# Attention score matmuls on 64-row halves of the TensorE array, per head, with a single K copy

## What is computed

```python
x = x + attn0(layernorm(x))        # 16 heads of width 8, softmax(q k^T / sqrt(8)) v, then @ wo.T + bo
x = x + ffn0(layernorm(x))         # silu(x wg^T) * (x wu^T), hidden 384, then @ wd^T (int weights / 127)
x = x + attn1(layernorm(x))        # 16 heads of width 8; q and k RMS-normalised per head and scaled
x = x + moe1(layernorm(x))         # x @ base_w^T + b + softmax-gated LoRA experts (8 experts, rank 8)
```

## Time and profile before

| | us |
|---|---|
| time, median of 3 runs (2163.48 to 2167.84) | 2164.41 |
| span of the profiled execution | 2165.0 |
| busy TensorE, its weight loads | 1980.4, 763.2 |
| busy VectorE, ScalarE, GpSimd | 1638.9, 1431.8, 434.7 |
| chain that ended last: PE 62%, issue 15%, DVE 10%, DMA 5%, POOL 4% | |
| busy share of the 16 DMA engines by the main queue | 23.2% |

### The profile page before, as it was taken

One profiled execution on the slowest core, in us unless ns is written; L12 is line 12 of the kernel. 1 busy time (PEld: TensorE's weight loads), 2 busy tenths in 40 slices (PEclk: granted clock), 3 DMA queues, 4 the chain that ended last, 5 costly groups with the idle time before them and its releaser, 6 DMA issues.

```text
span 2165.0 us, 38228 instructions
## 1 busy us (share of the span) xinstructions
PE 1980.4 (91%) x10706; PEld 763.2 (35%) x10706; DVE 1638.9 (76%) x3602; ACT 1431.8 (66%) x2921; POOL 434.7 (20%) x571
## 2 busy tenths in 40 slices
PE   3958999999999999999999999999999999999785
PEld 1223333333333333333333333333333333333332
DVE  5638888787887878778787877878787778888471
ACT  2615676676766767676776767677676767676643
POOL 2112121131212113121211312121121213121200
PEclk8858999999999999999999999999999999999977
DMA  5112314040311404031130404114050412302020
GB/s 108 55 25 58 87 34 122 18 135 19 111 44 39 116 17 137 17 116 39 46 109 17 138 16 119 36 46 109 17 138 17 118 36 62 94 20 72 18 63 16
DMA packets 162656, 140.94 MB, mean 65 GB/s; under 512 B 38761, under 2 KB 144050, under 8 KB 162482
## 3 DMA queue, kind: packets, MB, share of 16 engines
q1 hardware_dynamic: 162482, 139.29, 23.2%
HBM read 77.38 MB, written 55.57 MB: 61 GB/s over the span
## 4 chain that ended last, share of the span: by engine, by line
PE 62%; issue 15%; DVE 10%; DMA 5%; POOL 4%; ACT 2%; SPq 2%; DVEq 0%; POOLq 0%; ACTq 0%
PE ps L1159 17%; PE ps L1134 14%; PE ps L1144 14%; DVE neg_max L881 5%; PE ps L1209 4%; PE ps L1110 3%; PE ps L1173 3%; PE ps L1182 2%; PE ps L1214 2%; DMA k_stack<-k_rows 2%; ACT probs L661 1%; DVE bn L858 1%; DMA k_rows<-kp 1%; PE ps L1221 1%; DMA rden_all<-rden_rows 1%
## 5 line engine op out<-in xcount | busy, mean ns | idle before, releaser
L881 DVE TENSOR_REDUCE neg_max<-ps 128x1 f32<-128x512 f32 x2048 | 1323.5, 681 | 231.2 <-PE ps L1134 194.0
L661 ACT ACTIVATE probs<-ps 128x512 f32<-128x512 f32 x2048 | 1093.8, 599 | 347.2 <-PE ps L1144 345.6
L1134 PE MATMUL ps<-k_stack,q_stack 96*128 96x512 bf16 x2048 | 798.7, 392 | 80.2 <-DVE neg_max L881 51.2
L1144 PE MATMUL ps<-q_stack,k_stack 128*128 128x512 bf16 x2048 | 782.7, 385 | 16.8 <-ACT probs L661 14.0
L1159 PE MATMUL ps<-probs,v_aug 128*32 128x512 f32 x4096 | 548.8, 608 | 0.4
L1144 PEld LDWEIGHTS ps<-q_stack,k_stack 128*128 128x128 bf16 x2048 | 202.9, 100 | 441.8 <-ACT probs L661 244.9
L1134 PEld LDWEIGHTS ps<-k_stack,q_stack 96*128 96x128 bf16 x2048 | 202.3, 99 | 371.7 <-DVE neg_max L881 192.4
L561 POOL TENSOR_TENSOR o_raw<-o_raw,rden_all 128x512 f32<-128x512 f32 x64 | 81.4, 1272 | 580.7 <-DMA rden_all<-rden_rows 580.7
L1159 PEld LDWEIGHTS ps<-probs,v_aug 128*32 128x32 f32 x4096 | 80.7, 108 | 184.4 <-ACT probs L661 102.3
L667 ACT ACTIVATE xn<-x,shift,rstd 128x128 f32<-128x128 f32 x192 | 80.7, 486 | 49.4 <-POOL shift L544 49.3
L578 POOL TENSOR_TENSOR ht<-up,gs 128x512 f32<-128x512 f32 x48 | 60.9, 1268 | 257.3 <-ACT up L642 257.3
(11 more groups left out here) (109 smaller groups left out, 1487.5 us busy)
## 6 DMA issues: line engine op xcount, KB each, us to landing
q_stack<-q_rows SPq DMA_DIRECT2D x128, 192.0 KB, 3.4
k_stack<-k_rows SPq DMA_DIRECT2D x128, 192.0 KB, 4.3
rden_all<-rden_rows SPq DMA_DIRECT2D x64, 256.0 KB
q_rows<-qp SPq DMA_DIRECT2D x32, 384.0 KB, 2.6
k_rows<-kp SPq DMA_DIRECT2D x32, 384.0 KB, 3.0
q_rows<-qp SPq DMA_DIRECT2D x32, 256.0 KB, 2.9
k_rows<-kp SPq DMA_DIRECT2D x32, 256.0 KB, 3.0
x_in<-in_L_attn_x SPq DMA_DIRECT2D x16, 256.0 KB, 2.8
```

The source lines that it names most:

```text
L661: act.activation(probs[:, u % RING, :], ps[:, bank_of(l, u), :], ACT.Exp).then_inc(exps, 1)
L881: dve.tensor_reduce(neg_max[l][:, pair // 2, col:col + 1], ps[:, BANKS + bank_of(l, n), :], AX.X, ALU.max, negate=True).then_inc(max_taken, 1)
L1134: pe.matmul(ps[:, BANKS + bank_of(l, 2 * n + e), :], q_stack[l][0:QROWS, pair, tok:tok + 128], k_stack[l][e][0:QROWS, pair, :], start=True ...
L1144: pe.matmul(ps[:, bank_of(l, u), :], k_stack[l][e][:, pair, tok:tok + 128], q_stack[l][:, pair, :], start=True, stop=True).then_inc(scores, 1)
```

## The change

- One K copy: `k_stack[l]` holds head e = 0 in rows 0 to 49 (48 and two rows of ones) and head e = 1 in rows 64 to 113; `q_stack[l]` likewise, with each head's maximum rows behind its own 48.
- A score matmul reads only its head's rows: 48 (max) or 50 (attend), from row 0 or from row 64. The max units take e = 1 first, the attend units e = 0 first, so the halves alternate in TensorE's order: A low, M high, A high, M low.
- The zeroing and the ones rows on VectorE go; GpSimd fills both K stacks with bfloat16 ones (two memsets, at the start of its queue).
- `max_rows` needs two DMAs, one per head, and `m_in` counts 32 for each quarter.
- The pieces can be issued in parts, but `sub_slots` gives all parts of a piece the same half-step, behind the second score pair of the step as before. Only the form of q0, k0, g and u changes: two matmuls of 256 columns in the place of one of 512 (float32, each two instructions).

```diff
+ONE_PAIR = 1.001937866210937500
-QROWS = 2 * KROWS
+AROWS = KROWS + MROWS
+HALF = 64
...
+PARTS_OF = {"q0": 2, "k0": 2, "v0": 2, "v1": 2, "rt": 2, "pr0": 4, "pr1": 4, "dn": 4, "out": 4, "qka": 2, "qkb": 2,
+            "g0": 2, "u0": 2, "g1": 2, "u1": 2, "g2": 2, "u2": 2}
+
+def sub_slots(name, at_step):
+    n = PARTS_OF[name] if name in PARTS_OF else 1
+    return [(2 * at_step + 1, k, k == n - 1) for k in range(n)]
...
-        k_stack = [[sb(f"k_stack{l}{e}", [128, PAIRS, SEQ], BF16) for e in (0, 1)] for l in (0, 1)]
+        k_stack = [sb(f"k_stack{l}", [128, PAIRS, SEQ], BF16) for l in (0, 1)]
...
-                        sp.dma_start(stacks[e][KROWS * e:KROWS * e + KROWS, 4 * half:4 * half + 4, :], src
+                        sp.dma_start(stack[HALF * e:HALF * e + KROWS, 4 * half:4 * half + 4, :], src
                                      ).then_inc(stack_in[l][half], 16)
...
-                sp.dma_start(q_stack[l][QROWS:QROWS + 2 * MROWS, 2 * quarter:2 * quarter + 2, :],
-                             m_parts[l][quarter % 2][:, :]).then_inc(m_in[l][quarter], 16)
+                for e in (0, 1):
+                    sp.dma_start(q_stack[l][HALF * e + KROWS:HALF * e + AROWS, 2 * quarter:2 * quarter + 2, :],
+                                 m_parts[l][quarter % 2][16 * e:16 * e + 16, :]).then_inc(m_in[l][quarter], 16)
...
             pool.memset(mid_bias[:, EXPERTS:], 0.0)
+            for l in (0, 1):
+                pool.memset(k_stack[l][:, :, :].rearrange("p a b -> p (a b)").bitcast(F32), ONE_PAIR).then_inc(k_ones, 1)
...
-                        for t in (*k_stack[1], q_stack[1]):
-                            pool.memset(t[:, :, :].rearrange("p a b -> p (a b)").bitcast(F32), 0.0).then_inc(k_zeros, 1)
...
-                    zero_stacks((*k_stack[0], q_stack[0]))
                     place_weights()
-                    set_ones(0)
                     clear_values(0)
...
                                 clear_values(1)
-                                dve.wait_ge(k_zeros, 3)
-                                set_ones(1)
...
-                pair, st, e = n // 8, (n // 2) % 4, n % 2
+                pair, st, e = n // 8, (n // 2) % 4, 1 - n % 2
...
+            def max_score(l, m, b):
                 base = 2 * STEPS * maxima_before(l, b)
+                n, e = m // 2, 1 - m % 2
+                if m % 32 == 0:
+                    pe.wait_ge(stack_in[l][m // 32], 64 * (b + 1))
+                need(pe, max_taken, free_at(l, m, b, base))
+                tok, pair, row = 128 * (n % 4), n // 4, HALF * e
+                pe.matmul(ps[:, BANKS + bank_of(l, m), :], q_stack[l][row:row + KROWS, pair, tok:tok + 128],
+                          k_stack[l][row:row + KROWS, pair, :], start=True, stop=True).then_inc(max_scores, 1)
...
-                pe.matmul(ps[:, bank_of(l, u), :], k_stack[l][e][:, pair, tok:tok + 128],
-                          q_stack[l][:, pair, :], start=True, stop=True).then_inc(scores, 1)
+                tok, pair, row = 128 * kt, 2 * group + pp, HALF * e
+                pe.matmul(ps[:, bank_of(l, u), :], k_stack[l][row:row + AROWS, pair, tok:tok + 128],
+                          q_stack[l][row:row + AROWS, pair, :], start=True, stop=True).then_inc(scores, 1)
...
+            def by_column(w, xt, half):
+                return pe.matmul(gen[:, 256 * half:256 * half + 256], w, xt[:, 256 * half:256 * half + 256],
+                                 start=True, stop=True)
```

More of the change, by code:

```diff
@@ L423, in stack_half @@
                     hold(scores, UNITS * attends_before(l, b - 1) + 32 * (half + 1))
-                for rows, stacks in ((q_rows[l], (q_stack[l], q_stack[l])), (k_rows[l], k_stack[l])):
+                for rows, stack in ((q_rows[l], q_stack[l]), (k_rows[l], k_stack[l])):
                     for e in (0, 1):
@@ L1168, in turn_norm, with by_token @@
                 return last
-            def by_token(dst, xt, w, more=None):
-                for t in range(TT):
+            def by_token(dst, xt, w, tiles, more=None):
+                for t in tiles:
                     last = pe.matmul(dst[:, t, :], xt[:, 128 * t:128 * t + 128], w, start=True, stop=more is None)
@@ L1176, in by_token, with project, piece @@
                 return last
-            def project(l, b):
-                pe.wait_ge(att_ready[l], 2 * b + 2)
-                for t in range(TT):
-                    for c in (0, 1):
-                        last = pe.matmul(gen4[:, t, :], o_raw[l][:, c, 128 * t:128 * t + 128], wo[l][:, c, :],
-                                         start=c == 0, stop=c == 1)
+            def by_column(w, xt, half):
+                return pe.matmul(gen[:, 256 * half:256 * half + 256], w, xt[:, 256 * half:256 * half + 256],
+                                 start=True, stop=True)
+            def project(l, t):
+                for c in (0, 1):
+                    last = pe.matmul(gen4[:, t, :], o_raw[l][:, c, 128 * t:128 * t + 128], wo[l][:, c, :],
+                                     start=c == 0, stop=c == 1)
                 return last
-            def piece(name, i, at, kind, b):
+            def piece(name, k, i, at, kind, b):
                 before = piece_before(kind, at, name)
-                if before is not None:
+                if k == 0 and before is not None:
                     pe.wait_ge(read[sem_name(before[0])], count(before[0], i + before[1]))
@@ L1192, in piece @@
                 elif name in ("q0", "k0"):
-                    pe.wait_ge(read["xt0"], b + 1)
-                    last = pe.matmul(gen, (wq if name == "q0" else wk)[:, :], xnt[0][:, :], start=True, stop=True)
+                    if k == 0:
+                        pe.wait_ge(read["xt0"], b + 1)
+                    last = by_column((wq if name == "q0" else wk)[:, :], xnt[0], k)
                 elif name == "v0":
-                    pe.wait_ge(read["xt0"], b + 1)
-                    last = by_token(gen4, xnt[0], wv[:, :])
+                    if k == 0:
+                        pe.wait_ge(read["xt0"], b + 1)
+                    last = by_token(gen4, xnt[0], wv[:, :], (2 * k, 2 * k + 1))
                 elif name == "v1":
-                    last = by_token(gen4, xnt[2], wqkv[:, 256:384])
+                    last = by_token(gen4, xnt[2], wqkv[:, 256:384], (2 * k, 2 * k + 1))
                 elif name[0] == "m":
@@ L1235, in piece @@
                 elif name == "out":
-                    last = by_token(gen4, xnt[3], w_base[:, :], more=(coef_t, w_lora[:, :]))
-                last.then_inc(written[sem_name(name)], 1)
+                    last = by_token(gen4, xnt[3], w_base[:, :], (k,), more=(coef_t, w_lora[:, :]))
+                return last
             def slot(kind, i, at):
@@ L1249, in slot @@
                             pe.wait_ge(read["k0"], 1)
-                            last = by_token(gen4, xnt[0], wv[:, :])
+                            last = by_token(gen4, xnt[0], wv[:, :], range(TT))
                         else:
```

103 lines of the change are left out of this document (43 added, 60 removed).

## The result

The changed kernel takes 2136.26 us (median; 2124.73 to 2143.32) where the kernel before, on the same chip, takes 2165.45 (2163.48 to 2167.84): a ratio of 0.986, 95% interval 0.9825 to 0.9889. It is 29 us faster; I had forecast 91. The profiled executions have spans of 2134.1 and 2165.0 us, a difference of 30.9.

A forecast was written before the change was run, and what follows sets the result against it. TensorE's order of issue was taken as the bound, VectorE close behind. Steady turns 72 us (5.0 each), start 6.7, Y 0 5.4 and ends 7 sum to 91 off 2165: 2073 us; range 2035 to 2165, the forecast's own 2035 to 2110.

The forecast's parts named there:

- Halves do not overlap: Rival: a score pair keeps 0.44 us and 46 drains a turn come on top; 2201 us, chance 0.12.
- The ring does not bind: Rival: the three score banks hold nothing up, each group costs its most loaded engine's sum; 1980 us, chance 0.07.
- dearer drains and more chain waits: Rival: pairs overlap, but whole-array/halves changes cost 0.2 us (2146 us), or DMA chains wait more; 2110 to 2170, chance 0.12.
- start and Y 0: VectorE's memsets for the K copies go: stack loads 6.7 us earlier, first Y slot's gate product 5.4 us earlier.
- (a): Eight light groups a turn: 0.36 us each less what VectorE's or a piece's small work fills; 1.4 us together.
- (b): Ten groups a turn with a piece behind PV, Y 4 and X 9 included: 0.06 to 0.26 us each, 1.8 together.
- (c): Four groups a turn with pieces at both steps (Y 7, 8, 9, 13): 0.3 us each, 1.2 together.
- (d): Eight groups a turn that VectorE paces already (Y 5, 6, 11, 12, 14, 15, X 6, 7): nothing gained.
- (e): X 0 and X 1, at the loop's turn: X 0 loses a 0.1 drain, X 1 saves 1.05; 0.95 us together.
- 0.4 for the projection pr0: Layer-0 projection in Y: 0.23 us of slack before a DMA chain getting only part of the gain; 0.4 lost a turn.
- second DMA, I take 0: Extra issue of 0.69 us on SP per quarter of the maxima: cost taken as 0, other end 20 us.
- the clock: Rival: TensorE, less busy, gets a lower clock; one more low stretch a turn would be 25 us; chance 0.03.

The follow-up runs named there:

- The run without overlap: Changed kernel with every score matmul on the low half of the rows, head 1's scores left out: 2303.64 and 2335.93 us.
- The runs without the chain: Both kernels with GpSimd multiplying by a constant tile, waiting only for the denominators' first DMA: 2095.56 us from the changed kernel, 2149.55 from the kernel before.
- the waits moved in both kernels: Reciprocal's rows issued earlier, GpSimd's layer-1 residuals reordered, second half of layer 1's stacks later: changed kernel 2107.23 us, kernel before 2151.62.

## Why the prediction was right, and where it was wrong

**Right, the mechanism.** Pairs at 0.22 to 0.23, starting together; the fourth pair held by the ring of three (I had named the maximum; the exponential holds it too, 963.06); a light group 2.55 where I had 2.48; score to PV still 0.31. *Halves do not overlap* was the rival that would have made the kernel slower. The run without overlap is slower, but not as I had priced it: by medians its turn is 0.8 longer than that of the kernel before (65.0 + 61.2 against 63.4 + 62.0), where I had 3.4 for the drains, and what makes it slow is a low clock that I had not priced. *The ring does not bind* falls by the earlier trace rows's counterpart: by it the fourth pair starts 0.66 behind the first, and its two scores started at 1.15 and 1.24.

**Right, the drains.** PV to a piece stays 1.00 and a piece to the next score grew by 0.09 to 0.12 (an up projection from 0.96 to 1.06, the layer-0 projection from 1.89 to 1.98), by 0.20 for one (v1, 0.89 to 1.09). So the change between whole array and halves costs about what I took; four instructions in the place of two showed nothing more. The measured time lies in the band of the rival *dearer drains and more chain waits* (2110 to 2170, chance 0.12): of its two halves the drains are out, and the chain waits came.

**Right, start and Y 0.** The first attend score came at 55.8 and not 62.4, 6.6 (6.7 predicted); slots Y 0 and X 0 together are 6.0 shorter (5.4 predicted, and a part of the 7 for the ends), and the slot behind them 0.7. The rest of those 7 did not come: what follows the steady part is 1.5 longer, with 12 us more at 1.2 GHz.

**The groups,** by medians a turn: (a) 1.33 (1.4 predicted); (b) without Y 4 and X 9 1.55 of 1.8; (c) 0.98 of 1.2, since Y 9 gave nothing; (d) 0.9 where I had 0, since Y 14, X 6 and X 7 gained 0.3 each and so were not paced by VectorE alone; (e) 0.35 of 0.95, noisy since it hangs on where the low clock falls. All but Y 4 and X 9 give 5.1 a turn; the sum of the prediction, before it took 0.4 for the projection, was 5.35 with those two in it. That the total fits so well is in part luck, since (d) made up for (c) and (e). The range of 2035 to 2110 does not follow from the 3 to 8 us a turn beside it, which give 2102 and 2029; nothing hangs on that.

**Wrong, the term "0.4 for the projection pr0".** I read 0.23 us of slack ahead of "a chain of DMAs that gets only part of the gain" and priced the loss at 0.4 a turn. It gets none of it: the normalisation starts 13.9 us into the slot as before, and everything that the groups in front of it gained (0.3 + 0.2 + 0.4 + 0.2) comes back as a stand, and the projection lies in a low stretch in 6 of 13 slots. This is the step of the prediction that failed. Y 4 lost 1.4 by the median, 1.8 by the mean: 20 to 26 us in 14.5 turns. The runs without the chain show 25.

**Wrong, the term "second DMA, I take 0".** I looked at who waits for the maxima, and they had time. The cost is with those queued behind: the reciprocal's rows go out 8.6 us into the Y slot in place of 8.5, although VectorE's reciprocal starts at 6.9 in place of 7.5. In the kernel before alone it is 10 us, and moving one issue ahead of it brings 17 in the changed kernel. It is part of the same Y 4, and of X.

**Missing, the K stack at X 9.** The same shape: a chain through ScalarE, GpSimd and two DMAs (the second 4.6 us to land) that keeps its length (20.9 us before and 21.1 after, from the transposition of k to the score that waits), 18 us of waits more in the steady part. I had checked the projection for it and not this wait, which already held 6.1 us in 8 places in the kernel before.

**Wrong, the clock.** I gave it a chance of 0.03, "no reason", from a window of attend-only groups at full clock. There were 9 low stretches in the steady part and now there are 33. Two estimates of the loss agree. The mean turn of the changed kernel is 1.6 us above its median one, that of the kernel before 0.2 below: 1.9 a turn, some 26 us, most of it in Y 4, Y 6, Y 12, X 1 and X 9, where the stretches fall. And over the four executions of the changed kernel the mean granted clock rises from 0.923 to 0.942 while the time falls by 18.6 us; at that rate the step from 0.956 (before) to 0.934 (after) in the profiled executions is some 22 us. Neither shows that the clock is the cause, since longer waits could lower it and cost time of their own.

**Where the missing time stands.** Over the 14 steady turns 70 us were forecast and 19 came. The medians of Y 4 and X 9 hold 1.9 a turn, 26 us, and the difference of means and medians another 26; the ends hold 7 more. That says where, not why, and the causes overlap: with the waits moved in both kernels the change is worth 44, with the denominators' chain out of both 54. The 91 were not reached by any run, and the last 37 to 47 us I can name (K stack, clock, ends) but did not separate.

The Trainium skill (TensorE: Matmul & The Clock Gate, Part 1: The HAM clock gate) ties the clock to how busy TensorE has been, and I set that aside because the busy share stayed high. The trace of the changed kernel agrees in part: 22 of its 33 stretches at 1.2 GHz stand behind stands of 0.9 to 2.0 us, and the 6 at the projection went when its stand was filled. The other 11 stand behind less, and the 37.5 us at 1.2 GHz with TensorE's row busy throughout, in the kernel with all scores on one half, does not fit that simply.

## What to carry to other kernels

When a change shortens the work of the bounding engine evenly, list every wait of that engine that already ends with little or no slack, and price the whole gain of the groups in front of it as lost there: chains of DMAs and helpers run on their own time, and a queue's extra issue is paid by whoever is queued behind, not by the transfer's own reader. Then look at the clock again, since a new stand of TensorE can bring some microseconds at half speed behind it, and taking one stand away can move them to the next place instead of ending them. Reordering what feeds the waits was worth as much here as the change itself (29 us each), and only after it did the change show 44.

## What the hardware showed that I had not expected

- Matmuls on the two row halves start within 0.01 us of each other and the pair costs 0.22 to 0.23, what one costs.
- 3.41 us at a granted clock of 0.50 behind stands of 1.2 to 1.5 us: the projection's 16 instructions take 3.61 in such a stretch and 2.05 outside. But 11 of 33 stretches had no stand above 0.8 us in the 3 us before them, and with the projection's stand halved the low clock came to the same 130 us in other places.
- A kernel whose scores all sit in one half was at 1.2 GHz for 490 of 2334 us, and TensorE's row was busy for all of one stretch of 37.5 us; why, no run here tells.
- Filler work of 1.39 us a slot: 25 us slower where TensorE had no stand; where it had one, no loss, and 21 faster by medians that are not clear of noise.
- Three fillers at the loop's turn, and at 8 of 11 turns TensorE stood 4.2 to 4.9 us for nothing that the profile shows.
